# Attention and feed-forward kernel: the reciprocal of the row sums moves from GpSimd's power to VectorE's reciprocal

## The reference, cut to what matters

```
scores = einsum('bsgqd,btgd->bgqst', q, k) / sqrt(128)
scores = where(causal, scores, min)
attn   = softmax(scores, axis=-1)        # exp(s - max) / sum(exp(s - max))
out    = einsum('bgqst,btgd->bsgqd', attn, v)
```

## Time and profile before

| | |
|---|---|
| median of 3 runs | 979.06 us (978.54 to 979.51) |
| the profiled execution | 979.04 us, its span 977.2 us |
| granted PE clock, mean | 0.997 |
| busy share of the span | PE 97%, PEld 83%, DVE 67%, ACT 53%, POOL 48% |

### The profile page before, as it was taken

One profiled execution on the slowest core, in us unless ns is written; L12 is line 12 of the kernel. 1 busy time (PEld: TensorE's weight loads), 2 busy tenths in 40 slices (PEclk: granted clock), 3 DMA queues, 4 the chain that ended last, 5 costly groups with the idle time before them and its releaser, 6 DMA issues.

```text
span 977.2 us, 14506 instructions
## 1 busy us (share of the span) xinstructions
PE 947.1 (97%) x5344; PEld 816.0 (83%) x5344; DVE 653.1 (67%) x1290; ACT 516.6 (53%) x1085; POOL 467.7 (48%) x603
## 2 busy tenths in 40 slices
PE   6899999999999999999999999999999999999997
PEld 5688888888898889888988898889888987888885
DVE  6777657775777577757775777567757776864553
ACT  2466646664666466646664666466646665331221
POOL 3665646564556455545654565456545656120000
PEclk9999999999999999999999999999999999999999
DMA  8000000100010001000000010001000020000000
GB/s 313 24 1 33 2 22 1 33 1 22 1 33 2 22 1 33 1 23 1 33 1 22 1 33 1 22 1 34 1 1 1 1 87 1 1 8 15 21 21 21
DMA packets 9666, 21.92 MB, mean 22 GB/s; under 512 B 1280, under 2 KB 5504, under 8 KB 9472
## 3 DMA queue, kind: packets, MB, share of 16 engines
q1 hardware_dynamic: 8736, 20.45, 6.2%
q10 hardware_dynamic: 864, 0.60, 0.2%
HBM read 18.96 MB, written 2.10 MB: 22 GB/s over the span
## 4 chain that ended last, share of the span: by engine, by line
PE 80%; DVE 9%; ACT 5%; POOL 3%; issue 2%; DMA 1%; SPq 0%; DVEq 0%; POOLq 0%; ACTq 0%
PE ps L801 17%; PE ps L803 16%; PE ps L802 16%; PE ps L924 10%; PE ps L903 6%; PE ps L909 6%; PE ps L906 6%; ACT prob L487 2%; POOL rinv L373 2%; DVE pt_lo L706 2%; POOL prob L378 2%; DVE xhat L614 1%; DVE ps L702 1%; PE ps L825 1%; DVE v_lo L681 1%
## 5 line engine op out<-in xcount | busy, mean ns | idle before, releaser
L706 DVE TENSOR_TENSOR pt_lo<-ps,pt_hi 128x512 fp32r<-128x512 f32 x288 | 198.0, 690 | 101.7 <-ACT pt_hi L506 98.9
L506 ACT ACTIVATE pt_hi<-ps 128x512 fp32r<-128x512 f32 x288 | 171.0, 597 | 134.1 <-PE ps L924 132.6
L373 POOL TENSOR_TENSOR rinv<-rsum,mone 128x1 f32<-128x1 f32 x256 | 140.7, 550 | 211.5 <-ACT prob L487 210.7
L378 POOL TENSOR_SCALAR prob<-prob,rinv 128x1024 f32<-128x1024 f32 (+7 forms) x256 | 192.2, 751 | 53.3 <-POOL rinv L373 53.3
L487 ACT ACTIVATE prob<-ps,nmax 128x1024 f32<-128x1024 f32 (+7 forms) x256 | 189.5, 741 | 50.0 <-DVE nmax L702 48.3
L702 DVE CUSTOM_DVE_ANT_0 ps<-ps,mask_f 128x1024 f32<-128x1024 f32 (+7 forms) x256 | 192.9, 765 | 21.8 <-PE ps L909 19.5
L924 PE MATMUL ps<-ident,prob 128*128 128x128 f32 x1152 | 175.1, 273 | 6.2 <-DVE pt_lo L706 3.6
L924 PEld LDWEIGHTS ps<-ident,prob 128*128 128x128 f32 x1152 | 140.3, 140 | 36.8 <-DVE pt_lo L706 10.9
L801 PE MATMUL ps<-pt_hi,v_hi 128*128 128x512 f32 x288 | 132.5, 460 | 1.3 <-DVE pt_lo L706 0.5
L803 PE MATMUL ps<-pt_hi,v_lo 128*128 128x512 f32 x320 | 126.3, 395 | 0.0
L903 PE MATMUL ps<-k_hi,q_hi 128*128 128x512 f32 (+4 forms) x384 | 117.6, 360 | 0.0
(11 more groups left out here) (134 smaller groups left out, 1575.8 us busy)
## 6 DMA issues: line engine op xcount, KB each, us to landing
w_raw<-in_wqkv SPq DMA_DIRECT2D x9, 768.0 KB, 4.2
wp_raw<-in_wproj SPq DMA_DIRECT2D x8, 512.0 KB, 3.5
x<-in_x SPq DMA_DIRECT2D x4, 512.0 KB, 9.8
prob<-in_wug SPq DMA_DIRECT2D x4, 512.0 KB, 5.3
out_y<-prob SPq DMA_DIRECT2D x4, 512.0 KB, 3.0
prob<-in_wmod SPq DMA_DIRECT2D x1, 1024.0 KB, 9.7
raw_down<-in_wdn SPq DMA_DIRECT2D x1, 1024.0 KB, 14.1
prob<-in_wmod SPq DMA_DIRECT2D x1, 512.0 KB, 5.2
```

The source lines that it names most:

```text
L378: g_.tensor_scalar(row, row, rinv[:, s % 2, h:h + 1], 1.0, ALU.mult, ALU.mult).then_inc(prob_done, 1)
L506: a_.activation(pt_hi[:, n % 3, :], T[n % 2], ACT.Copy).then_inc(pth_done, 1)
L706: v_.tensor_tensor(pt_lo[:, n % 3, :], T[n % 2], pt_hi[:, n % 3, :].bitcast(F32), ALU.subtract).then_inc(ptl_done, 1)
```

## The change

The power on POOL goes, with its constant. DVE takes a reciprocal of the same column instead. It keeps a list `summed` of the heads whose maximum it has taken, and empties it behind the next maximum (before the new head is entered) and behind each low part `pt_lo`. Before each reciprocal DVE waits for the exponential of that head. POOL waits for `rinv_done`, which DVE now signals, and scales.

```diff
-        mone = sb("mone", [P, 1])
...
-        PER_DVE = {qkv_lo: 10, v_lo_s: 2, max_done: 32, ptl_done: NU, ol_done: NT, add_done: NT}
-        PER_POOL = {prob_done: 32, rinv_done: 32}
+        PER_DVE = {qkv_lo: 10, v_lo_s: 2, max_done: 32, rinv_done: 32, ptl_done: NU, ol_done: NT, add_done: NT}
+        PER_POOL = {prob_done: 32}
...
-            g_.memset(mone[:, :], -1.0)
...
-                            pool.wait_ge(exp_done, this(exp_done, t, e + 1))
-                            g_.tensor_tensor(rinv[:, s % 2, h:h + 1], rsum[:, s % 2, h:h + 1], mone[:, :],
-                                             ALU.pow).then_inc(rinv_done, 1)
                             pool.wait_ge(rinv_done, this(rinv_done, t, e + 1))
...
+                    summed = []
+
+                    def reciprocals(keep):
+
+                        while len(summed) > keep:
+                            s, h = summed.pop(0)
+                            dve.wait_ge(exp_done, this(exp_done, t, QPG * s + h + 1))
+                            v_.reciprocal(rinv[:, s % 2, h:h + 1], rsum[:, s % 2, h:h + 1]).then_inc(rinv_done, 1)
...
                             v_.tensor_tensor_reduce(row, row, late, -1.0, 3.0e38, ALU.add, ALU.min,
                                                     nmax[:, s % 2, h:h + 1]).then_inc(max_done, 1)
+                            reciprocals(0)
+                            summed.append((s, h))
                         if what == "T":
                             dve.wait_ge(pth_done, this(pth_done, t, n + 1))
                             v_.tensor_tensor(pt_lo[:, n % 3, :], T[n % 2], pt_hi[:, n % 3, :].bitcast(F32),
                                              ALU.subtract).then_inc(ptl_done, 1)
+                            reciprocals(0)
```

## The result

The changed kernel takes 983.04 us (median of 7 runs, 982.16 to 983.64), the kernel before 979.06 (7 runs, 978.54 to 979.95). The ratio is 1.0039, 95% interval 1.0028 to 1.0051: 4.0 us more. The forecast was 983.6.

The account below looks back on a forecast made before the run. PE, busy 97% of the span, was taken as the bound. Turn starts cost 7.9 us and block 1's lost POOL wait gains 3.3: + 4.6 on 979.04 gives 983.6 us, own range 981.2 to 986, overall range 976 to 988.

Parts of the forecast that it names:

- only two places of a turn: Where the change can act on PE: a late POOL-scaled row near a turn's end, units 3 and 4's `pt_lo` waits near its start.
- T4: Unit 4's transposes near a turn's start, waiting for unit 2's `pt_lo`: 0.99 us later, 8 x 0.99 = 7.9 us cost.
- The gain, 0.41 us a turn: Block 1, unit 0's transposes: PE's wait for POOL's fourth scaled head should go, 8 x 0.41 = 3.3 us.
- The 960 us case: Rival on the chain by line: the power's 19 us come off the end, giving 960 us; chance under 1%.
- The count by the weight load's wait: Alternative count of PE's block 1 wait for POOL: 4.2 us in all, against 2.3 by the matmul.
- (7,3): Block 7 head 3's reciprocal, behind block 6's first maximum: its scaled row comes late, stalling PE's unit 0 transposes about 1.15 us.
- d = 0.14: At a turn's start, us by which ACT's `pt_hi` of unit 0 is late, what lasts of PE's 1.15 us stall.
- r = 0.14: On DVE, us by which one added reciprocal holds up the next instruction; possible from nothing to 0.18.
- (6,1)'s wait: DVE's reciprocal for block 6 head 1 waits for ACT's exponential until 257.99; the next maximum starts 1.17 us late.
- The lower blocks at nothing: DVE's similar waits below a turn's start, 0.6 us late in block 6, cost PE nothing; 8 us if cover failed.
- Only the gain is real: Rival: the turn-start stall is swallowed, block 1's POOL wait goes, 975.7 us; needs block 6's third maximum by about 257.2; 14%.
- the even case: Rival: a turn's start costs only some 0.4 us, so the time stays at 979 to 980 us; chance 14%.

Follow-up runs that it names:

- experiment 1: Kernel before without the power and without any reciprocal, POOL scaling by the sum itself (output not the softmax's): 974.75 us, 0.9951 of before.
- experiment 2: Kernel before, power kept on POOL, plus DVE's waits for exponentials at the change's places, without reciprocals: 985.0 us, 1.006 of before.
- experiment 3: Changed kernel with block 7 head 3's reciprocal moved from behind the next block's first maximum to behind C9's low part: 980.17 us, 1.0008 of before.
- experiment 4: Changed kernel with block 6 head 1's reciprocal moved from behind unit 1's low part to behind the next maximum: 978.93 us, 0.9997 of before.
- experiment 6: The hybrid: POOL takes the power as in the kernel before in blocks 7 and 6, DVE the reciprocal in blocks 5 to 0: 975.16 us, 0.9963.
- experiment 7: Kernel before, power kept on POOL, plus 256 DVE reciprocals of a constant at the change's places, without waits: 979.76 us, 1.0007 of before.
- the order with two reciprocals moved: Changed kernel with the reciprocal moves of experiment 3 and experiment 4 together: 976.1 us, 0.9969 of before.

## Why the prediction was right

The verdict, the place and the mechanism were right, and the time was 0.6 us off. Some of that closeness is luck: two terms of the cost missed in opposite directions, and by the turns the change costs 3.4 us, not the forecast's 4.6 (most of what separates the 3.4 from the medians' 4.0 is the clock, below). Point by point, with what each term measured:

- **The bound.** PE sets the time, and only two places of a turn matter. Right: with T4 laid over T4 the two kernels' PE runs alike for 53.17 us.
- **The gain, 0.41 us a turn.** Measured 0.47 in the rows, 0.53 by experiment 1's turn and 0.55 by its median. The step that was too large is the 0.11 us for one more transpose, taken from durations: four transposes keep PE for 0.35 us (416.09 to 416.44, and 252.44 to 252.79), 0.09 each, so the fourth could have started about 0.26 us after the first, and not 0.33. Where in a turn the last 0.06 us are gained was not found. The 960 us case is out by experiment 1. The count by the weight load's wait, 4.2 us in all, came nearest to the 4.2 (turns) and 4.4 (medians) measured.
- **(7,3) and d = 0.14.** The stall was 1.12 (forecast 1.15). d was 0.30: ACT's `pt_hi` started at 256.45 - 2.03 = 254.42 instead of 254.12. The steps that were too small are the hand-overs. POOL ended at 256.03 - 2.03 = 254.00 instead of near 253.9 (its start came 0.20 us after the reciprocal's end, 254.71 to 254.91), the transpose started 0.06 us behind it and `pt_hi` 0.03 us behind the transpose, both of which had been put at nothing. The 0.33 us of the single transpose were as forecast.
- **r = 0.14.** It was 0.07 and 0.08 (257.69 to 257.76, 260.06 to 260.14), so the full 0.18 us is out as well. The two misses, d too small and r too large, nearly cancel: d + r was 0.37 against a forecast 0.28, and the second r gave 0.06 back.
- **(6,1)'s wait.** The reciprocal started at 260.06 - 2.03 = 258.03 (forecast 257.99), the next maximum at 258.11 (258.13), the low part at 259.11 (259.14).
- **T4.** + 0.95 against + 0.99. 8 x 0.95 - 8 x 0.47 = 3.8 us; the medians say 4.0, the turns 3.4, the forecast said 4.6. Experiments 2, 3 and 4 show the pieces by themselves, by the turn and by the median: the wait 0.68 and 0.73 us a turn, the late T0 0.30 and 0.36, the order of (6,1) 0.45 and 0.51.
- **The lower blocks at nothing.** Right, by experiment 6.
- **The rivals.** "Only the gain is real" fell at T4's wait, as its own condition had it: the maximum of (6,2) would have had to start by 257.2 and started at 258.11. Of the even case nothing was seen.

One thing in the two traces is not the change's: the first T4 is 2.09 us late (61.38 to 63.47), and a turn's start accounts for 0.95 of it. The other 1.1 us are already there at the maximum of (7,1) in the first turn, before DVE's first reciprocal (before, then after):

```profile
44.36 1.23 DVE L702 CUSTOM_DVE_ANT_0 ps<-ps,mask_f 128x1024 f32<-128x1024 f32 x1
```

```profile
45.48 1.23 DVE L706 CUSTOM_DVE_ANT_0 ps<-ps,mask_f 128x1024 f32<-128x1024 f32 x1
```

PE's granted clock accounts for all of them but 0.2 us, by which PE's first work there already starts late (37.86 and 38.08). PE stands idle there for 3.7 us in the kernel before and 3.8 in the changed one, from 34.1 and 34.2 on, waiting for `xhat`. Then the clock falls from the upper of its two levels (2.4 GHz) to the lower (1.2 GHz): it is low from 38.6 to 42.0 us in the trace of before, when PE had just begun again, and from 36.8 to 43.7 us in the other, where PE was still idle. The same matmul near 42.5 us shows both levels (before, then after):

```profile
42.12 0.39 PE L801 MATMUL ps<-h_hi,w_hi 128*128 128x512 f32 x1
```

```profile
42.81 0.63 PE L808 MATMUL ps<-h_hi,w_hi 128*128 128x512 f32 x1
```

Executions of one and the same kernel differ by this much. Of the kernel before, beside experiments 1 to 4, seven executions with a mean clock of 0.995 took 979.75 to 980.34 us and fourteen with 0.997 or 0.998 took 978.83 to 979.57. Of the changed kernel four took 983.04 to 983.64 at 0.995, and three 982.16 to 982.38 at 0.997 or 0.998. Compared at like clocks the change costs 3.3 us (0.997 and 0.998) and 3.7 us (0.995). That is nearer to the turns' 3.4 than the 4.0 of the medians, which mix the two. Why the low level lasts longer in some executions is open.

## What to carry to other kernels

Moving a small operation to an engine with free time is not a matter of its duration: ask what it waits for there, and what is queued behind it. Here 40 us of instructions cost 0.3 us (experiment 7) and the waits alone 5.8 us (experiment 2), because the maximum and the low part queued behind one of them, of 0.77 us in the turn shown, fed the engine that was the bound. Put such an operation behind the instruction that the bound engine needs next, or leave it where it was in the few places where that can't be done: the hybrid took 975.16 us and the order with two reciprocals moved 976.1, both faster than either kernel.

## What the runs showed that I had not expected

- Idle time of the busiest engine is no measure of loss. PE idles 9.0 us at T0 in the changed kernel. Taking all of that away gave 2.9 us (experiment 3; 2.4 by the turns), and leaving all of it in place still allowed 978.93 us (experiment 4).
- A one-column reciprocal on DVE takes 161 ns but holds up the next instruction by only 0.07 to 0.08 us, less than the 142 ns of a read-out suggested.
- A hand-over between engines is not one number: ACT's read-out to DVE's reciprocal took 0.03 us (260.03 to 260.06 in the timelines), DVE's reciprocal to POOL's scaling 0.20 us.
- The clock at the start moves a median here. 3.4 us less or more of PE at the lower level made 1.1 us between two traces, a quarter of what the change costs. A distance between two like rows of one trace, taken behind that stretch, is free of it.
